# Cross-attention on one core: turning the probabilities by halves of the array's rows

## The reference

```python
D_Q, D_CTX, N_HEADS, HEAD_DIM = (256, 192, 16, 64)
h = _layernorm(x, gamma, beta)                      # x: (8, 256, 256)
Q = (h @ Wq).reshape(B, NQ, N_HEADS, HEAD_DIM)      # context: (8, 256, 192)
K = (context @ Wk).reshape(B, NC, N_HEADS, HEAD_DIM)
V = (context @ Wv).reshape(B, NC, N_HEADS, HEAD_DIM)
attn = jnp.einsum('bihd,bjhd->bhij', Q, K)
attn = jax.nn.softmax(attn, axis=-1) * scale        # scale = 64 ** -0.5
vals = jnp.einsum('bhij,bjhd->bihd', attn, V).reshape(B, NQ, INNER)
out = x + vals @ Wo + bo
```

## Time and profile before

| | |
|---|---|
| median of 3 runs | 355.9 us (355.87 to 356.07) |
| profiled execution, its own time | 356.03 us |
| its span in the trace | 354.2 us |
| busy: TensorE matmuls | 344.2 us (97%), 3266 |
| busy: VectorE | 244.4 us (69%) |
| busy: ScalarE | 256.8 us (72%) |
| busy: GpSimd | 165.4 us (47%) |
| instructions | 9031 |

### The profile page before, as it was taken

How to read it: one execution, slowest core, us unless ns; L and a number is a source line. 1 busy time by engine, 2 the same in 40 slices (tenths; PEclk the granted TensorE clock), 3 DMA queues, 4 the chain that set the end, 5 groups by cost and what they waited for, 6 DMA issues and landing times.

```text
span 354.2 us, 9031 instructions
## 1 busy us (share of the span) xinstructions
PE 344.2 (97%) x3266; PEld 306.7 (87%) x3266; DVE 244.4 (69%) x534; ACT 256.8 (72%) x800; POOL 165.4 (47%) x321
## 2 busy tenths in 40 slices
PE   5989999999999999999999999999999999999986
PEld 5779888899888889988889988889988889988875
DVE  5897667866778667676677666776677856566654
ACT  4898877776778766878667877777777876677762
POOL 4576994227453264443642455322745325444331
PEclk9999999999999999999999999999999999999999
DMA  6940010020000100020000200002000000000000
GB/s 181 279 135 3 1 54 2 3 81 2 3 0 33 53 0 2 2 81 2 3 2 0 83 2 0 2 2 81 2 2 0 31 2 2 0 4 31 2 2 30
DMA packets 10756, 10.61 MB, mean 30 GB/s; under 512 B 960, under 2 KB 10176, under 8 KB 10720
## 3 DMA queue, kind: packets, MB, share of 16 engines
q1 hardware_dynamic: 10192, 9.64, 8.7%
q10 hardware_dynamic: 416, 0.33, 0.3%
q0 software_dynamic: 112, 0.13, 0.2%
HBM read 8.00 MB, written 2.10 MB: 28 GB/s over the span
## 4 chain that ended last, share of the span: by engine, by line
PE 91%; ACT 4%; DVE 2%; POOL 1%; issue 1%; DVEq 0%; POOLq 0%; ACTq 0%
PE mix_ps L745 16%; PE st_ps L862 15%; PE o_ps L834 12%; PE w_ps L809 12%; PE st_ps L716 12%; PE w_ps L769 10%; PE w_ps L896 8%; PE w_ps L909 3%; ACT prob L421 2%; PE w_ps L787 1%; PE mix_ps L699 1%; PE mix_ps L691 1%; ACT qk_hi L431 0%; DVE w_lo L507 0%; PE o_ps L686 0%
## 5 line engine op out<-in xcount | busy, mean ns | idle before, releaser
L333 POOL TENSOR_SCALAR prob<-prob,inv 128x256 f32<-128x256 f32 x256 | 121.1, 490 | 149.6 <-DVE inv L587 149.6
L421 ACT ACTIVATE prob<-st_ps,neg_max 128x256 f32<-128x256 f32 x256 | 118.9, 479 | 23.5 <-DVE neg_max L580 23.5
L580 DVE TENSOR_REDUCE neg_max<-st_ps 128x2 f32<-128x512 f32 x128 | 82.0, 684 | 26.2 <-PE st_ps L716 25.4
L475 ACT ACTIVATE prob_t<-st_ps 128x512 f32<-128x512 f32 x64 | 38.4, 601 | 37.9 <-PE st_ps L862 37.9
L660 DVE COPY prob_t<-st_ps 128x512 f32<-128x512 f32 x64 | 44.2, 691 | 26.2 <-PE st_ps L862 22.8
L745 PE MATMUL mix_ps<-prob_t,v_sb 128*64 128x256 f32 x504 | 61.5, 385 | 0.1
L862 PE MATMUL st_ps<-ident,prob 128*128 128x128 f32 x512 | 61.1, 272 | 0.0
L862 PEld LDWEIGHTS st_ps<-ident,prob 128*128 128x128 f32 x512 | 56.5, 141 | 0.1
L593 DVE TENSOR_TENSOR qk_lo<-w_ps,qk_hi 128x512 fp32r<-128x512 f32 x62 | 42.8, 691 | 17.6 <-ACT qk_hi L431 17.6
L421 ACT ACTIVATION_READ_ACCUMULATOR prob<-st_ps,neg_max 128x1 f32 x256 | 53.9, 211 | 0.0
L745 PEld LDWEIGHTS mix_ps<-prob_t,v_sb 128*64 128x64 f32 x504 | 33.4, 136 | 17.9 <-issue 0.3
(11 more groups left out here) (139 smaller groups left out, 654.6 us busy)
## 6 DMA issues: line engine op xcount, KB each, us to landing
x_in<-in_x_dram SPq DMA_DIRECT2D x8, 256.0 KB, 3.0
out_dram<-y_sb SPq DMA_DIRECT2D x7, 256.0 KB, 2.1
c_in<-in_ctx_dram SPq DMA_DIRECT2D x7, 192.0 KB, 2.8
w_raw<-in_L_xattn_Wq_dram SPq DMA_DIRECT2D x8, 128.0 KB, 3.5
w_raw<-in_L_xattn_Wo_dram SPq DMA_DIRECT2D x4, 256.0 KB, 4.1
w_raw<-in_L_xattn_Wk_dram SPq DMA_DIRECT2D x4, 128.0 KB, 4.0
w_raw<-in_L_xattn_Wk_dram SPq DMA_DIRECT2D x8, 64.0 KB, 3.5
w_raw<-in_L_xattn_Wv_dram SPq DMA_DIRECT2D x2, 256.0 KB, 4.2
```

The source lines that it names most:

```text
L333: last = nc.gpsimd.tensor_scalar(prob[:, e, r, :], prob[:, e, r, :], inv[:, e, r:r + 1], SCALE, ALU.mult, ALU.mult)
L421: last = nc.scalar.activation(prob[:, e, r, :], st_ps[e][:, r * ROWS:(r + 1) * ROWS], ACT.Exp, bias=neg_max[:, e, r:r + 1], accum_out=sums ...
L475: nc.scalar.activation(prob_t[:, e, :, :].rearrange("p a b -> p (a b)"), st_ps[e][:, :], ACT.Copy)\
L580: nc.vector.tensor_reduce(neg_max[:, e, :], st_ps[e][:, :].rearrange("p (r j) -> p r j", r=RT), AX, ALU.max, negate=True).then_inc(max_rea ...
```

## The change

A step's turn is cut into 32 transposes of 64 rows in place of 16 of 128. For a pair of heads (a = 0, 1) and each of its eight blocks (head h, context half j, row half r, counted by k), rows 0 to 63 of the block are turned into bank `st_ps[2a]` and rows 64 to 127 into `st_ps[2a+1]`, 64 columns each, from the upper and the lower row half of the array. So a bank holds no longer one head, but one half of the rows of two heads. The turn waits for `scaled` once a pair of heads instead of once a head, and both banks of a pair are counted `turned` at the pair's end. The copies out, one a bank as before, put their 512 columns into `prob_t` as eight runs of 64 with gaps of 64 (`turned_half`), so that `prob_t` is laid out as it was. The place of the turn in the step and who copies what bank number stay.

```diff
--- before.py
+++ after.py
@@ -1,6 +1,7 @@
 import concourse.bass as bass
 from concourse import mybir
 from contextlib import ExitStack
+import itertools
 
 
 def cross_attention_block(nc, x, ctx_in, w_q, w_k, w_v, w_o, b_o, gamma, beta, out):
@@ -124,6 +125,11 @@
             if i < O0:
                 return (w_lo, w_hi)[high][:, i, c0:c1]
             return (wo_lo, wo_hi)[high][:, i - O0, c0:c1]
+
+        def turned_half(e):
+
+            pair = prob_t[:, e // 2 * 2:e // 2 * 2 + 2, :, :]
+            return pair.rearrange("p h j (r x i) -> p (h j r) x i", x=2, i=HALF)[:, :, e % 2, :]
 
         def qk_banks(u):
 
@@ -472,8 +478,8 @@
                         act.wait_ge(mixed, u + turns(8))
                     for e in range(0, HEADS, 2):
                         act.wait_ge(turned, HEADS * u + e + 1 + turns(32))
-                        nc.scalar.activation(prob_t[:, e, :, :].rearrange("p a b -> p (a b)"),
-                                             st_ps[e][:, :], ACT.Copy)\
+                        nc.scalar.activation(turned_half(e), st_ps[e][:, :]
+                                             .rearrange("p (k i) -> p k i", i=HALF), ACT.Copy)\
                             .then_inc(prob_t_ready[0], 1)
                         if u == 0 and e == 0:
                             weight_hi(12)
@@ -657,8 +663,9 @@
                         dve.wait_ge(mixed, u + turns(8))
                     for e in range(1, HEADS, 2):
                         dve.wait_ge(turned, HEADS * u + e + 1 + turns(32))
-                        nc.vector.tensor_copy(prob_t[:, e, :, :].rearrange("p a b -> p (a b)"),
-                                              st_ps[e][:, :]).then_inc(prob_t_ready[1], 1)
+                        nc.vector.tensor_copy(turned_half(e), st_ps[e][:, :]
+                                              .rearrange("p (k i) -> p k i", i=HALF))\
+                            .then_inc(prob_t_ready[1], 1)
                         if u == 0 and e == 1:
                             weight_lo(13)
                 b = of_seq(u, TURN_C, 2)
@@ -855,14 +862,17 @@
                             last.then_inc(o_added, 1)
 
             def turn(u):
-                for e in range(HEADS):
-                    pe.wait_ge(scaled, HEADS * u + e + 1)
-                    for r in range(RT):
-                        for j in range(RT):
+
+                for a in range(BATCH):
+                    pe.wait_ge(scaled, HEADS * u + 2 * a + 2)
+                    for k, (h, j, r) in enumerate(itertools.product(range(2), range(RT), range(RT))):
+                        for half in range(2):
+                            own = slice(half * HALF, (half + 1) * HALF)
                             last = nc.tensor.transpose(
-                                st_ps[e][:, j * ROWS + r * P:j * ROWS + (r + 1) * P],
-                                prob[:, e, r, j * P:(j + 1) * P], ident[:, :])
-                    last.then_inc(turned, 1)
+                                st_ps[2 * a + half][:, k * HALF:(k + 1) * HALF],
+                                prob[own, 2 * a + h, r, j * P:(j + 1) * P], ident[own, own])
+                            if k == 2 * RT * RT - 1:
+                                last.then_inc(turned, 1)
 
             def values(n):
```

## The result

The changed kernel takes 344.12 us (median of 4, 344.1 to 344.21) against 355.9: the ratio is 0.9664, with a 95% interval of 0.9652 to 0.9676. It is 11.8 us faster where 11.7 us slower was forecast, outside the range of 361 to 373. The span is 342.4 us.

The account below looks back on a forecast made before the run. TensorE was taken to bound the kernel. Terms 1.0 + 6.2 + 4.5 = 11.7 us on the median of 355.9 gave 367.6 us, mechanism range 365 to 372.5; 361 to 373 was to hold 0.8.

Parts of the forecast that it names:

- Halved transposes: In the turn, 16 pairs at 0.111 us each replace 16 transposes at 0.109: +1.0 us over 32 steps.
- The holes: TensorE drains at the two added changes of array shape, going into and out of the turn: +6.2 and +4.5 us.
- the coarser wait: The turn waits for scaled probabilities once per head pair: cost 0, some 0.1 us once in steps 0 and 1.
- The stated bounds: Whole kernel: 365 to 372.5 us, with the pair at 0.105 or 0.118 and the last flow at 0.03 or 0.11.
- The rival that came true: In the turn, half the rows load in half the time, a pair takes 0.055 us: 339 us, chance 0.09.
- the copies at today's price: Copies out of the turn in runs of 64 keep 0.60 us (ScalarE) and 0.69 us (VectorE): cost 0.
- the readers of `prob_t` not late: The next scores, reading the turned probabilities, needn't wait: 1.0 us covers the second pair of copies, cost 0.
- the halves side by side: In the turn, two row halves load and flow beside one another, as score pairs do at 0.115 to 0.12 us.
- the matmul record of about 220: In the turn, transpose matmul records shorten by the halved flow, from 272 to about 220 ns.
- the holes' places: TensorE idle without a releaser in front of the turn and in front of lines 896, 691 and 699.
- the rounds of four steps: Four steady steps together go from 42.19 to about 43.65 us.

Follow-up runs that it names:

- experiment 2: Changed kernel with one whole 128 x 128 transpose added between the two pairs of heads each step: 356.54 us, 12.4 more than the changed kernel.
- experiment 1: Kernel before with only 64 of each transpose's 128 stationary columns loaded, all 128 identity columns still moving: 356.04 us against 356.04, ratio 1.0002.
- experiment 3: Kernel before with its 16 transposes a step made as ordinary fp32 matmuls with the identity: 413.2 us in a single run.
- experiment 4: Changed kernel with only 64 of the 128 stationary columns of each block loaded, 64 moving columns as before: 340.85 us.
- experiment 6: Kernel before with only heads 2 and 3 turned in halves: 355.71 us, ratio 0.9991; F is the fixed price of the shape changes.
- experiment 5: Changed kernel with each head pair's eight upper halves before its eight lower: 356.81 us; a second kernel, all sixteen upper before all sixteen lower: 382.28 us.

## Why the prediction was wrong

**The step that failed** is in *Halved transposes*: "each load still has 128 stationary columns, 0.105 ... So a pair can't be under the load's 0.105". The 0.105 came from line 909 and the 0.051 from line 745, both loads for matmuls. It was carried over to loads for transposes, for which neither row speaks. There 128 columns take 0.052 to 0.058 (the changed kernel's first pairs and experiment 2), experiment 1 shows that the load was hidden before, and experiment 3 ties the difference to the transpose. The pair takes 0.062 where 0.111 was taken: 16 x (0.062-0.109) x 32 = -24 us in place of +1.0. Why it is 0.062 and not the 0.055 of the flow is open (experiment 4).

**What the trace of before would have shown.** The load records of line 862 lasted 141 ns and those of line 716, with as many columns, 184 to 186: a gap of the very size in question. And one transpose with its load uncovered stood there too, the very first of line 686 (the identity turned by itself). It lasts 477 ns and all others of the line 421, at a time when a transpose took longer than the later 272, so 128 columns took 0.056:

```profile
L862 PEld LDWEIGHTS st_ps<-ident,prob 128*128 128x128 f32 x512 | 56.5, 141 | 0.1
L716 PEld LDWEIGHTS st_ps<-qk_lo,qk_hi 64*128 64x128 f32 x256 | 24.2, 184 | 0.0
L686 PE MATMUL o_ps<-ident x12: 421/421/477, 3.8 to 7.0; 128*128 128x128 f32 x12
```

The prediction read the matmul records of other lines only.

**The holes were nearly right.** Forecast were 6.2 + 4.5 = 10.7 us. In the step shown, from the last output matmul to the first flowing column of the values it is 163.56 to 164.91+0.105 = 165.02, 1.46 us, where before it was 168.36 to 170.23 (line 896 started at 170.14 and lasted 0.09 over the usual), 1.87. Of this -0.41 the 15 distances between pairs are 15 x (0.062-0.109) = -0.70. The way in, from the last output matmul to the first flow of the turn, grew from 0.11 to 0.26, and the way out, from the last start to the flow behind it, from 0.12 to 0.26. So the holes are +0.29 a step, about 9.1 us in all: the forecast less the 1.7 by which the load uncovered in front of the turn, 0.05 and not 0.105, was put too high. The 11.3 of experiment 6 agree with that, since its F also holds the 16th pair, behind which stands the hole and no distance of 0.062 (0.047 x 32 = 1.5 us), and the output stage's 0.9 us of the next paragraph.

**Terms put at nothing.** The output stage's matmuls stand 0.118 apart in 29 of steps 1 to 30 of the changed kernel, but in only 9 of them before, where the others have 0.114: 0.9 us over the trace, and why is open. And the coarser wait was to cost some 0.1 us once; in steps 0 and 1 it costs 0.8. Together: 32 x (-0.41) + 0.9 + 0.8 = -11.4 us, against -11.8 measured. The stated bounds don't follow from their own terms either: 355.9-1.9+6.2+3.7 = 363.9 and 355.9+4.6+6.2+6.2 = 372.9, not 365 and 372.5; the measured time is outside of both.

**The rival that came true** is the first, at a chance of 0.09, by its mechanism of pairs under 0.088 but not by its reason: the load doesn't shrink with its rows (0.052 for 64, 0.058 for 128). It gave 339 by 0.055 a pair; with 0.062 it would have given 0.007 x 512 = 3.6 more, 342.6. That it came within 5 us is in part luck: its load of 0.055 for half the rows is by chance about what a transpose's load of any rows takes.

**Right besides:** the copies at today's price; the readers of `prob_t` not late; the coarser wait nearly free in the steady steps; the halves side by side, which experiment 5 shows to be needed; the matmul record of about 220; the holes' places. Wrong with the main term: the rounds of four steps (43.65 forecast, 40.55 measured).

## What to carry to other kernels

A price read from one kind of instruction held for that kind only: before a load, a flow or a copy is put down as a floor, look at the records of the very group that is changed, and at whether they are as long as those from which the price was taken. Where two costs lie over one another (here 0.109 of flow over 0.05 of load), a change that halves the visible one gains until the hidden one shows, so the hidden one must be measured and not bounded by a relative. And changes of the array's split into row halves are paid per change and not per instruction: 0.29 us for the pair of them here, so that halving 8 of 16 transposes gained nothing, and halving all 16 gained 11.8 us.

## What the runs showed of the hardware beyond that

- A transpose's load takes 0.052 us (64 rows) and 0.058 (128 rows) for 128 fp32 columns at the 2.4 GHz level, where a matmul's load of 128 columns takes 0.105. The Trainium skill (TensorE: Matmul & The Clock Gate, LDWEIGHTS) has one rule for both, the columns over 1.2, which gives 107 ns; the measurement decides, and it agrees for matmuls only.
- A stage of 128*64 in the first 64 columns, between two of 128*128, made no hole (experiment 1), while the mix, whose 128*64 matmuls use both column halves, has one on either side. The form in the records alone doesn't tell a change of split. Whether the use of both column halves makes the difference, or that one stage is transposes and the other is not, no run separates.
- Halves written as eight upper and then eight lower ones did not run one after the other: the lower ones began 0.30 us after the first upper one, and three of them started before the eighth upper one (experiment 5).
